# State-space layer on one core: VectorE turns x and B of every chunk to tokens, and the freed PSUM bank joins the rotation of the dense units

## What is computed

```python
xn = _layernorm(x)
# branch 1, H=64 heads of P=64, state N=128, G=8 groups, I=4096
proj = xn @ in_proj_w.T                      # gate (4096), x, B and C (4096+1024+1024), dt (64)
xBC = silu(causal convolution of 4 taps over the tokens)
dt = softplus(dt + dt_bias); dA = exp(-exp(A_log) * dt)
state_t = state_(t-1) * dA_t + (dt_t * x_t) outer B_t;   y_t = state_t . C_t
y = y + x * D
y = rmsnorm over each group of 512 channels * norm_weight * silu(gate)
branch1 = y @ out_proj_w.T
# branch 2: xn @ W_base.T + b_base + a low-rank term of the top 2 of 8 experts
out = x + branch1 + branch2
```

## Time and profile before

| | us |
|---|---|
| median of 3 executions | 3176.2 (3176.06 to 3176.92) |
| the profiled execution, its own time | 3177.18 |
| its span, first to last instruction | 3175.3 |
| PE busy | 3157.5 (99%) |
| DVE busy | 2469.2 (78%) |
| ACT busy | 1550.1 (49%) |
| POOL busy | 857.4 (27%) |

### The profile page before, as it was taken

The page is one execution under the profiler, slowest core; times in us unless marked ns, Lnnn a source line. Parts: engine busy times, 40 slices in busy tenths (PEclk is TensorE's granted clock), DMA queues, the critical chain, the costliest instruction groups (busy, mean ns, idle before and its releaser), DMA issues.

```text
span 3175.3 us, 55177 instructions
## 1 busy us (share of the span) xinstructions
PE 3157.5 (99%) x17933; PEld 2598.2 (82%) x17933; DVE 2469.2 (78%) x4773; ACT 1550.1 (49%) x3816; POOL 857.4 (27%) x917
## 2 busy tenths in 40 slices
PE   8999999999999999999999999999999999999999
PEld 7788888887888888888788888888878888888887
DVE  7977777786588888888658888888855888888883
ACT  5666656663364444454235544445423545444441
POOL 4444434343032222222102222222210222222220
PEclk9999999999999999999999999999999999999999
DMA  8777777776665555556476555556557655555554
GB/s 288 273 269 263 265 276 261 277 258 255 238 208 183 189 187 192 187 187 209 160 234 201 185 188 189 196 181 194 196 170 237 193 192 186 192 189 197 183 189 159
DMA packets 185666, 672.63 MB, mean 212 GB/s; under 512 B 21056, under 2 KB 22208, under 8 KB 185408
## 3 DMA queue, kind: packets, MB, share of 16 engines
q1 hardware_dynamic: 161280, 584.91, 54.6%
q10 hardware_dynamic: 24128, 84.42, 7.9%
HBM read 532.41 MB, written 136.84 MB: 211 GB/s over the span
## 4 chain that ended last, share of the span: by engine, by line
PE 95%; DVE 3%; ACT 1%; DMA 1%; issue 0%; SPq 0%; ACTq 0%; DVEq 0%
PE dense L1040 27%; PE dense L1042 27%; PE dense L1041 27%; PE pY L1140 3%; PE pD L1170 2%; PE pD L1140 1%; DVE conv_us L1452 1%; PE pCB L1116 1%; PE pU L1040 1%; PE dense L1077 1%; PE pS L1041 1%; PE pS L1040 1%; PE pU L1042 1%; PE pS L1042 1%; PE pU L1041 1%; PE pX L1110 1%
## 5 line engine op out<-in xcount | busy, mean ns | idle before, releaser
L1040 PE MATMUL dense<-xn_hi,w_hl 128*128 128x512 f32 (+1 forms) x2888 | 1143.2, 396 | 1.4 <-POOL w_hl L437 0.8
L1042 PE MATMUL dense<-xn_hi,w_hl 128*128 128x512 f32 (+1 forms) x2888 | 1125.1, 390 | 0.0
L1041 PE MATMUL dense<-xn_lo,w_hl 128*128 128x512 f32 (+1 forms) x2888 | 1123.6, 389 | 0.0
L1042 PEld LDWEIGHTS dense<-xn_hi,w_hl 128*128 128x128 f32 (+1 forms) x2888 | 540.1, 187 | 115.7
L1040 PEld LDWEIGHTS dense<-xn_hi,w_hl 128*128 128x128 f32 (+1 forms) x2888 | 540.7, 187 | 114.4 <-issue 3.0
L1041 PEld LDWEIGHTS dense<-xn_lo,w_hl 128*128 128x128 f32 (+1 forms) x2888 | 540.9, 187 | 110.9 <-issue 1.9
L1452 DVE SCALAR_TENSOR_TENSOR conv_us<-conv_in,const_g,conv_us 128x512 f32<-128x512 f32 x576 | 466.2, 810 | 138.8 <-ACT conv_us L686 123.2
L1040 PE MATMUL dense<-z_hi,w_hl 128*128 128x512 f32 x1024 | 406.0, 397 | 1.9 <-DVE acc L1606 1.4
L1042 PE MATMUL dense<-z_hi,w_hl 128*128 128x512 f32 x1024 | 399.3, 390 | 0.0
L1041 PE MATMUL dense<-z_lo,w_hl 128*128 128x512 f32 x1024 | 398.7, 389 | 0.0
L493 POOL TENSOR_TENSOR C_lo<-BC,C_hi 128x128 fp32r<-128x128 f32 x120 | 73.5, 613 | 1191.0 <-ACT S_hi L724 1190.3
(11 more groups left out here) (205 smaller groups left out, 4610.1 us busy)
## 6 DMA issues: line engine op xcount, KB each, us to landing
w_hl<-w_split SPq DMA_DIRECT2D x732, 512.0 KB, 3.5
w_split<-w_hl SPq DMA_DIRECT2D x244, 512.0 KB, 3.6
cum_b<-cum_scratch ACTq DMA_DIRECT2D x128, 512.0 KB, 5.0
w_raw<-w_slots_dram SPq DMA_DIRECT2D x122, 512.0 KB, 5.2
acc<-x_tr_dram ACTq DMA_DIRECT2D x16, 512.0 KB, 6.0
out_tr_dram<-acc ACTq DMA_DIRECT2D x16, 512.0 KB, 4.7
BC<-x_tok_dram SPq DMA_DIRECT2D x6, 512.0 KB, 5.0
conv_us<-x_tok_dram SPq DMA_DIRECT2D x6, 512.0 KB, 5.8
```

What stands on the lines that cost most here:

```text
L1040: nc.tensor.matmul(out, lhs[0], rhs[0], start=start, stop=False)
L1041: nc.tensor.matmul(out, lhs[0], rhs[1], start=False, stop=False)
L1042: return nc.tensor.matmul(out, lhs[1], rhs[0], start=False, stop=stop)
```

## The change

It does four things, in paired groups alone:

1. `BY_DVE` becomes (0, 1, 2, 3): the 4 PE transposes of x of chunk 1 go, DVE does them as 16 stream transposes.
2. `B_tm` gets four chunks, and `B_rows` turns all four in the same 16 stream transposes (32x128 in place of 32x96): the PE transpose of B of chunk 0 goes. `B_rows` of a group moves to the end of the group before: the first half behind the last unit's taps, ahead of `gated(g, 2)`; the second half behind `silu(5)`, ahead of `prep`. Behind the unpaired group 0 all of it stands ahead of `prep`. In its old place stand quarters of `x_rows(1)`.
3. `chunk_1_rest(1)` on DVE moves behind the first half of `out_adds(1)`.
4. Bank `pX`, now free of x, is a third bank: dense units of paired groups (and the tail of their block) take `pX`, `bank[1]`, `bank[0]` in turn, and PE waits for the evacuation three units back in place of two. The layer norm's transposes use `pS` where they used `pX`.

The diff, cut to its core (the same addition of `two=True` or `True` to calls of units is shown once):

```diff
-        B_tm = sb("B_tm", [128, NC - 1, N])
+        B_tm = sb("B_tm", [128, NC, N])
-        ln_banks = [pCB, pX, pU, pY]
+        ln_banks = [pCB, pS, pU, pY]
+        def turn_bank(unit):
+            return (pX, bank[1], bank[0])[unit % 3]
-        BY_DVE = (0, 2, 3)
+        BY_DVE = (0, 1, 2, 3)
 # ACT chunk_1
-                    if two and c > 0:
+                    if two:
                         act.wait_ge(bt_done, bt_n(q, g))
-                    nc.scalar.activation(B_hi[:], B_tm[:, c - 1, :] if two and c > 0 else pCB[:, 0:N], ACT.Copy).then_inc(ck_evac, 1)
+                    nc.scalar.activation(B_hi[:], B_tm[:, c, :] if two else pCB[:, 0:N], ACT.Copy).then_inc(ck_evac, 1)
 # PE
-                def gate_unit(g, first, j):
+                def gate_unit(g, first, j, two=False):
...
+                    if two and j == 0 and g == 1:
+                        pe.wait_ge(xd_done, chunk(q, 0, NC - 1) + 1 + 1)
+                    elif two:
+                        pe.wait_ge(evac_act, act_n(q, g - 1, 7 + j) if j < 3 else act_n(q, g, j - 3))
...
+                    in_unit(g, k, turn_bank(j) if two else bank[(k if first else k - 4) % 2])
 # PE out_units
-                        if i >= 2:
-                            pe.wait_ge(evac_dve, tail_n(q, i - 2) if tail else out_n(q, g, i - 2))
+                        ahead = 3 if two else 2
+                        if i >= ahead:
+                            pe.wait_ge(evac_dve, tail_n(q, i - ahead) if tail else out_n(q, g, i - ahead))
 # PE paired_group
-                    chunk_1(g, 0, p, 0 in BY_DVE, False)
+                    chunk_1(g, 0, p, True, True)
-                    out_units(g, 0)
-                    chunk_1(g, 1, p, 1 in BY_DVE, True)
+                    out_units(g, 0, two=True)
+                    chunk_1(g, 1, p, True, True)
 # DVE B_rows
-                            src = BT[p][32 * f:32 * f + 32, :].rearrange("n (c t) -> n c t", c=NC)[:, 1:NC, 32 * k:32 * k + 32]
+                            src = BT[p][32 * f:32 * f + 32, :].rearrange("n (c t) -> n c t", c=NC)[:, :, 32 * k:32 * k + 32]
 # DVE group (unpaired), at its end
+                        if not first_block:
+                            B_rows(g + 1, 1 - p, 0, 4)
                         prep(g + 1)
 # DVE paired_group
                     if last:
                         router_weights()
+                    x_rows(g, 1, p, 0, 1)
                     y_state(g, 0, True)
                     y_skip(g, 0, True)
                     gate_tile(g, 3, False)
                     state(g, 0)
                     dve.wait_ge(acc_loaded, (q + 1) * 64)
-                    B_rows(g, p, 0, 1)
-                    out_adds(g, 0, halves=(0,))
-                    B_rows(g, p, 1, 3)
-                    out_adds(g, 0, halves=(1,))
-                    B_rows(g, p, 3, 4)
+                    x_rows(g, 1, p, 1, 2)
+                    out_adds(g, 0, halves=(0,), two=True)
+                    x_rows(g, 1, p, 2, 4)
+                    out_adds(g, 0, halves=(1,), two=True)
                     if not last:
                         consts_next(g, p)
-                    chunk_1(g, 1, True)
-                    out_adds(g, 1, halves=(0,))
+                    chunk_1_x(g, 1, True)
+                    out_adds(g, 1, halves=(0,), two=True)
+                    chunk_1_rest(g, 1, True)
                     x_rows(g, 2, p, 0, 1)
...
                     x_unit(j_first + 5)
+                    if not last:
+                        B_rows(g + 1, 1 - p, 0, 2)
                     gated(g, 2)
                     save_state(g)
                     gated_lo(g, 2)
...
                         silu(g, 5, 1 - p)
+                        B_rows(g + 1, 1 - p, 2, 4)
                         prep(g + 1)
```

More of the change, by code:

```diff
@@ L692, in tanh_conv, with ev_gate @@
                     nc.scalar.activation(conv_in[j % 2][:, 0:TB], conv_u[j % 2], ACT.Tanh).then_inc(tanh_done, 1)
-                def ev_gate(g, first, j, p):
+                def ev_gate(g, first, j, p, two=False):
                     k = k_gate(first, j)
-                    b = (k if first else k - 4) % 2
+                    b = turn_bank(j) if two else bank[(k if first else k - 4) % 2]
                     act.wait_ge(dense_done, dense_n(q, g, k, 1))
@@ L774, in first_unit @@
                     split(0, K_FIRST + j)
-                    ev_conv(-1, K_FIRST + j, j, (1 + j) % 2, 1)
+                    ev_conv(-1, K_FIRST + j, j, bank[(1 + j) % 2], 1)
                     if j >= 1 and tanh:
@@ L835, in x_conv @@
                     def x_conv(j):
-                        ev_conv(g, K_X + j, j, (K_X + j) % 2, p)
+                        ev_conv(g, K_X + j, j, bank[(K_X + j) % 2], p)
                     def x_unit(j, z=None):
@@ L925, in x_unit @@
                             tanh_conv(g, j - 1)
-                        ev_conv(g, K_X + j, j, (K_X + j) % 2, p)
+                        ev_conv(g, K_X + j, j, turn_bank(12 + j), p)
                     gate_unit(0)
@@ L1076, in more, with out_units @@
                             pe.wait_ge(evac_dve, ffn_n(q, 0))
-                            return nc.tensor.matmul(bank[(K_X + j) % 2][:], lora_sb[:, (j - 1) * 128:j * 128], w_tok[:],
+                            return nc.tensor.matmul(b[:], lora_sb[:, (j - 1) * 128:j * 128], w_tok[:],
                                                     start=False, stop=True)
-                    in_unit(7, K_X + j, (K_X + j) % 2, more)
-                def out_units(g, m, tail=False):
+                    in_unit(7, K_X + j, b, more)
+                def out_units(g, m, tail=False, two=False):
                     k = (K_TAIL if tail else K_OUT) + m
@@ L1095, in out_units @@
                         weights(g, k, h)
-                        b = ((K_TAIL if tail else 3) + i) % 2
+                        b = turn_bank((0 if tail else 4) + i) if two else bank[((K_TAIL if tail else 3) + i) % 2]
                         for t in range(KZ):
-                            mm = three(bank[b][:], w(k, 4 * h + t), (z_hi[:, t, :], z_lo[:, t, :]), t == 0, t == KZ - 1)
+                            mm = three(b[:], w(k, 4 * h + t), (z_hi[:, t, :], z_lo[:, t, :]), t == 0, t == KZ - 1)
                         mm.then_inc(dense_done, 1)
@@ L1307, in paired_group @@
                     chunk_2y(g, 1, True)
[L1308 to L1309 removed]
+                    chunk_1(g, 2, p, True, True)
+                    out_units(g, 3, two=True)
                     x_units(2 if last else 1)
@@ L1518, in chunk_1_rest @@
                     nc.vector.tensor_tensor(CBm, pCB[:, N:N + Q], causal[:], ALU.mult).then_inc(cbm_done, 1)
-                    nc.vector.tensor_tensor(B_lo[:], B_tm[:, c - 1, :] if two and c > 0 else pCB[:, 0:N], B_hi[:].bitcast(F32), ALU.subtract)\
+                    nc.vector.tensor_tensor(B_lo[:], B_tm[:, c, :] if two else pCB[:, 0:N], B_hi[:].bitcast(F32), ALU.subtract)\
                         .then_inc(bl_done, 1)
@@ L1597, in gated_lo, with out_adds @@
                         .then_inc(z_done, 1)
-                def out_adds(g, m, tail=False, halves=(0, 1)):
+                def out_adds(g, m, tail=False, halves=(0, 1), two=False):
                     for h in halves:
@@ L1953, in paired_group @@
                     chunk_1_x(g, 2, True)
-                    out_adds(g, 3, halves=(0,))
+                    out_adds(g, 3, halves=(0,), two=True)
                     chunk_1_rest(g, 2, True)
-                    out_adds(g, 3, halves=(1,))
+                    out_adds(g, 3, halves=(1,), two=True)
                     masked(g, 2, True)
@@ L2017, in block_body @@
                 for m in range(4):
-                    out_adds(7, m, tail=True)
+                    out_adds(7, m, tail=True, two=not first_block)
                     if m < 2:
```

92 lines of the change are left out of this document (48 added, 44 removed).

## The result

The changed kernel takes 3185.48 us (3183.86 to 3186.55, median of 9), against 3176.44 (3174.32 to 3177.70) of the kernel before on the same chip: ratio 1.0029, interval 1.0019 to 1.0039. That is 9.0 us slower, where +3.3 was forecast; 3185.5 lies in the range of 3165 to 3191, which is 26 us wide. The span of the profiled execution went from 3175.3 to 3183.4 us.

The account below looks back on a forecast made before the run. PE's own work was taken to bound the kernel: - 11.4 (transposes gone) + 14.4 (waits at `pU`) + 0.3 (z) = + 3.3 us, 3180.5 on the profiled execution, 3179.5 as median; range 3165 to 3191.

Parts of the forecast that it names:

- PE's gain, 0.55 a group, 11.4 us: On PE, five transposes removed at 0.11 us each save 0.55 us per paired group, 11.4 us over 21 groups.
- Third bank worth 0, cover only: In paired groups PE never waits for evacuations, so the third bank gains 0 and only covers late `out_adds`.
- Relief of `dtx(0)` and `wx(0)`: On DVE at chunk 0, both no longer meet POOL: 1.3 us in place of 2.9, lateness falls from 3.5 to 1.9.
- Collision of `xD(1)` with `wx_lo(1)`: On DVE at chunk 1, `xD(1)` now waits for POOL's `wx_lo`: + 1.2 us, with bounds 0 and 1.9.
- Lateness at `gated(g, 0)`: DVE reaches `gated(g, 0)` 2.3 us late, after idle time has taken up 0.5.
- Rival 1: `xD(1)` and `wx_lo(1)` pass each other, PE waits for nothing, gain in full: 3165 to 3168 us; 27%.
- Rival 2: `dtx(1)` and `wx(1)` also held by POOL's chunk 1 work: 3190 us for one, 3200 for both; 20%.
- Rival 3: PE transposes cost their whole 272 ns, so removing 105 gives 28.6 us: 3148 us; 2%.
- The wait at `pU`, in 12 groups: PE's load for `pU` of chunk 3 waits 1.2 us in groups 1 to 6 of blocks 1 and 2: 14.4 us.
- These 9 groups keep their 0.55: Block 3 and group 7 lack the chain to `chunk_2b(3)`, so they lose nothing and keep 0.55 us each.
- Z, 0.3 us in all, 3 at most: At PE's first output unit, `gated_lo(g - 1, 3)` 1.9 late costs 0.0 to 0.1 us; 0.3 over 21 groups, at most 3.

Follow-up runs that it names:

- e1_two_banks: The changed kernel with all units going by two banks in place of three: 3220.24 us, ratio 1.0137 to the kernel before.
- e2_rest_back: The changed kernel with `chunk_1_rest(1)` put back ahead of the first output add of unit 1: 3168.72 us, ratio 0.9976 to the kernel before.
- e6_dose: The changed kernel with 4 stream transposes of chunk 2 made twice, 1.26 us more of DVE per group: 3288.92 us, ratio 1.0351 to the kernel before.
- e5_act_order: The changed kernel with ACT's `z_high(g, 1)` behind `chunk_1(3)` and DVE's `masked(3)` ahead of `gated_lo(1)`: 3174.21 us, ratio 0.9992 to the kernel before.
- e3_no_x1: The changed kernel without 15 of the 16 DVE transposes of x of chunk 1: 3168.20 us, ratio 0.9975 to the kernel before.
- e4_b_only: The changed kernel with only B moved to DVE; x of chunk 1 stays on PE, units use two banks: 3177.59 us, ratio 1.0004 to the kernel before.
- e12_z_first: e2_rest_back with `gated(g-1, 3)` ahead of `chunk_1_rest(0)` and `gated_lo(g-1, 3)` ahead of `masked(0)` on DVE: 3188.14 us, ratio 1.0038 to the kernel before.

## Why the prediction was right and wrong

- *PE's gain, 0.55 a group, 11.4 us*: right. Free of waits the groups are 89.00 and 88.32, 0.59 and 0.53 below before.
- *Third bank worth 0, cover only*: right, and e1_two_banks gives the cover its price, 34.8 us.
- *Relief of `dtx(0)` and `wx(0)`*: right, 0.69 and 0.68. *Collision of `xD(1)` with `wx_lo(1)`*: right, 1.78 where "near 1.9" was said; e2_rest_back shows that it decides the sign of the change. *Lateness at `gated(g, 0)`*: right, 2.4 (51.14 for 48.77) where 2.3 was said. Rival 1, the kernel without it, was put at 3165 to 3168 and is this experiment, 3168.7. Rival 2, a second collision, did not come: `dtx(1)` starts at 1232.37, 0.05 ahead of the end of POOL's `S_cur(1)` at 1232.42, and takes 0.68. It was close, and in e6_dose such collisions came, one chunk later. Rival 3 is answered by the 0.59 us of a group.
- *The wait at `pU`, in 12 groups*: place and number right, 0.66 each where 1.2 was taken (from the C by B product of chunk 3 to `pU` it is 12.47 for 11.81). The step that sized it, all of 1.2 us meeting PE there, missed that PE is stopped twice earlier: at z (0.17) and at `pD` of chunk 1 (0.18), whose transposes overwrite what `gated(g, 0)` reads. Each makes PE later and so leaves less lateness for the next wait. In sum the three and the 0.1 behind them are 1.1 us, and the groups took 90.12, for a forecast of 90.24 (89.59 - 0.55 + 1.2).
- *"These 9 groups keep their 0.55"*: wrong, this is the failed step. I looked for the one place where lateness meets PE, and where that was missing took the lateness as harmless. In block 3 it is harmful at z (0.36) and `pD` (0.29), more than elsewhere: 88.99 for 88.3, 6 groups, 4.0 us. Why more, is open: one could say that no wait at `pU` holds PE back there, but e5_act_order has no such wait in blocks 1 and 2 either, and loses no more at z and `pD` for it. In group 7 `w_tok`, which the first low-rank product waits for, stands behind the late list of DVE: 26.99 for 26.13, and with z 181.53 where 180.45 would have kept the gain (the transpose of B lies in the cut ahead), and 0.3 more in block 3: 3 groups, 3.5 us.
- *Z, 0.3 us in all, 3 at most*: mis-sized, the sum of what the first cuts have above 18.44 is 4.5 us: 2.0 in the 12 groups, 1.8 in the six of block 3, 0.7 in the groups 7. The step that failed is DVE's lateness at that place. In the medians of groups 2 to 6 `dtx(0)` starts 6.85 us behind the C by B product of chunk 0, for 3.09 before: 3.8 late, not 3.5. `z_lo` ends 12.96 behind it, for 10.81: 2.15 late, not 1.9. That it is no effect of PE's other waits, e2_rest_back, e3_no_x1 and e4_b_only show: they have none of those at `pU` and `pD`, and the same 6.85 and 12.96.

Put into the sum: 3.3 + 4.0 + 3.5 - 12 x 0.12 = 9.4, and 8.1 in the spans. Of the 1.3 between, 0.3 is z counted twice; some 0.4 is that group 1 of blocks 1 and 2 takes 89.9 and not 90.12; and 0.6 lies ahead of block 1, which starts that much earlier than before (870.34 for 870.96). That last part may well be chance: in the traces of the other kernels, with the same code there, block 1 starts between 869.8 and 870.9.

So the mechanism of the 12 groups was right and their sum nearly exact, and the other 9 groups, with 7.5 us, were wrong. That the result lies in the range owes much to the width of the range; the change itself is 2.7 times the forecast.

## What to carry over

When work moves onto an engine with slack, list every place where a faster engine waits for it, in its order, and carry the lateness through all of them: in stages where the wait that you found is absent, the lateness still meets the other places, and two cures of one wait do not add. Where two engines can block each other, look at starts to a tenth of a us: here an operation put 0.4 us ahead of its rival was free, and put 0.2 us behind it cost 1.1 us, nearly what was left of the rival's length, and a reorder by one short step is a cheap thing to try. The change as it stood was 9.0 us slower than the kernel before; the same change with three such reorders is 10.0 us faster.

## What the runs showed of the hardware

- A 128x512 DVE operation with both inputs in SBUF that started behind a running POOL operation of 128x128 or 128x512 waited for its end (it ended 0.55 us behind it each time: 1.78, 1.78 and 1.78 us in three kernels at three places), and one that started ahead took its 0.68. Behind POOL's 128x1 operations it did not wait: `dtx(2)` started 0.04 behind one (1247.97, 0.55 us long) and took 0.70. In the changed kernel 83 output adds and 28 `z_t`, which have an input in PSUM, and 408 stream transposes of x began while a POOL operation ran, and took their usual 0.67 to 0.69, 0.68 and 0.29 to 0.31. The Trainium skill, SBUF — State Buffer, Who interferes with whom, says that VectorE instructions with two SBUF inputs contend with a GpSimd instruction that reads SBUF, and that issue order decides who blocks; the rows agree on both, down to 0.18 behind against 0.43 ahead, the 128x1 operations apart.
- It holds the other way too. POOL's `S_lo` of chunk 2, begun 0.36 behind DVE's `wx` in the changed kernel, took 1.74 us, and `S_cur`, begun together with `xD`, 1.58; at other places they took 1.30 and 1.05:

```profile
1248.01 0.70 DVE L1525 TENSOR_TENSOR dtx<-x_tm,tok_g 128x512 f32<-128x512 f32 x1
1248.63 0.95 DVE L1528 TENSOR_TENSOR wx<-x_tm,tok_g 128x512 f32<-128x512 f32 x1
```
```profile
1248.99 1.74 POOL L497 TENSOR_TENSOR S_lo<-S_cur,S_hi 128x512 fp32r<-128x512 f32 x1
1250.80 1.58 POOL L501 TENSOR_TENSOR S_cur<-S_cur,tok_g 128x512 f32<-128x512 f32 x1
```

- A wait of PE of 3.4 us in e6_dose, behind a busy stretch at full clock (1.00 from 1225.29 to 1276.8), was followed by the 1.2 GHz level. The clock fell within the wait: 1.00 from 1276.8 to 1279.6, 0.52 up to 1280.6, 0.50 up to 1286.4, 0.99 from there to 1290. The mean of the execution is 0.983. e1_two_banks (0.998) has three waits of 2.4 us, one in each group 7, and each has such a stretch behind it: the first ends at 1508.94, and the granted clock is 0.52 from 1509.0 to 1512.5 and 1.00 behind that. e12_z_first, whose waits in the groups last 1.6 us at most, has none (mean 1.000).
- The slow stretch of e6_dose cost some 2.7 us more than the wait itself: 0.42 on the four transposes (0.91 from 1280.63 on, for 0.49 in the changed kernel) and 2.3 in the fourth cut, 39.30 against the 36.98 of a group without waits. From the windows, 5.8 us at half the clock would be 2.9, an estimate.
